# Graph network on one core: norms taken from columns in the node stages, and one difference for both exponents in the edge scan

## What is computed

```python
f = h + EPS
f = f * CLIP / jnp.maximum(CLIP, _norm(f))
fn = _norm(f)
p = jnp.tanh(fn) * f / fn
p = p + EPS
p = p * CLIP / jnp.maximum(CLIP, _norm(p))
Mp = p @ W
pn = _norm(p)
atan_norm = jnp.arctanh(jnp.clip(sqrt_c * pn, -0.9, 0.9))
t = Mp * atan_norm / pn / sqrt_c
t = t * clip2 / jnp.maximum(clip2, _norm(t))
tn = _norm(t)
hh = jnp.tanh(sqrt_c * tn) / sqrt_c / tn * t
...
g = hh + EPS
g = g * CLIP / jnp.maximum(CLIP, _norm(g))
gn = _norm(g)
log_h = jnp.arctanh(jnp.clip(sqrt_c * gn, -0.9, 0.9)) * g / gn
```

```python
seg_max = jax.ops.segment_max(logits, target, num_segments=m)
e = jnp.exp(logits - seg_max[target])
denom = jax.ops.segment_sum(e, target, num_segments=m)
out = jax.ops.segment_sum(e / denom[target] * (w3[source] + d), target, num_segments=m)
```

## Time and profile before

| what | value |
| --- | --- |
| time, median of 3 runs | 3100.99 us (3099.07 to 3108.09) |
| the profiled execution | 3096.49 us, its span 3094.6 us |
| `hyperbolic_nodes` | 563.0 to 666.4 us of the span |
| `end_hyperbolic` | 1293.2 to 1334.1 us |
| `edge_softmax` | 1619.0 to 2790.5 us |
| `end_edges` | 2790.5 to 2872.0 us |
| DVE, PE, ACT, POOL busy over the span | 74%, 61%, 59%, 34% |
| SP's queue in 1700 to 2700 us, waiting for the row copies | 453.9 us in 88 waits, at most 7.6 |

### The profile page before, as it was taken

One profiled execution on the slowest core, in us unless ns is written; L12 is line 12 of the kernel. 1 busy time (PEld: TensorE's weight loads), 2 busy tenths in 40 slices (PEclk: granted clock), 3 DMA queues, 4 the chain that ended last, 5 costly groups with the idle time before them and its releaser, 6 DMA issues. The chain is left out here.

```text
span 3094.6 us, 39006 instructions
## 1 busy us (share of the span) xinstructions
PE 1888.4 (61%) x7042; PEld 1007.8 (33%) x7043; DVE 2296.7 (74%) x4650; ACT 1832.1 (59%) x2352; POOL 1044.7 (34%) x984
## 2 busy tenths in 40 slices
PE   3354555359798567548846666666666666650636
PEld 1122222223333222112233434343433344430636
DVE  4799999479999678768926777777777777775444
ACT  0166666338888444358927877777777777860010
POOL 1000000000000011013207777777777777753000
PEclk8689898555656699869957777777777777765868
DMA  2144444104544499425614555555555555551616
GB/s 84 41 148 147 147 143 143 59 32 164 185 172 177 196 364 373 191 90 209 231 30 146 168 165 166 162 171 166 166 156 170 164 167 161 166 147 29 265 56 223
DMA packets 288619, 490.59 MB, mean 159 GB/s; under 512 B 39166, under 2 KB 237646, under 8 KB 275718
## 3 DMA queue, kind: packets, MB, share of 16 engines
q1 hardware_dynamic: 254694, 394.56, 36.7%
q0 software_dynamic: 26688, 54.65, 7.4%
q10 hardware_dynamic: 7200, 40.96, 3.4%
HBM read 282.58 MB, written 209.91 MB: 159 GB/s over the span
## 5 line engine op out<-in xcount | busy, mean ns | idle before, releaser
L1794 POOL DMA_INDIRECT es_got<-w,es_idx x808 | 882.3, 1092 | 346.1 <-issue 342.4
L1929 PE MATMUL en_pv<-en_sq,avg 128*128 128x512 f32 x202 | 197.7, 1079 | 371.6 <-ACT en_sq L2036 371.6
L1391 PE MATMUL acc<-src_hot,dst_hot 128*128 128x401 f16 x1008 | 231.6, 382 | 186.7 <-DVE src_hot L1366 166.7
L1366 DVE TENSOR_SCALAR src_hot<-iota,col_key 128x400 f16<-128x400 f16 x1008 | 315.9, 313 | 0.0
L1364 DVE TENSOR_SCALAR dst_hot<-iota_blk,row_key 128x128 f16<-128x128 f16 x1008 | 247.4, 245 | 11.9 <-PE acc L1391 11.4
L803 PE MATMUL pd_dn<-hT,pd_lhs 66*128 66x512 f32 (+1 forms) x350 | 233.3, 845 | 23.0 <-DVE pd_top L906 18.2
L2064 ACT COPY es_rows<-es_rp 128x512 f32<-128x512 f32 x202 | 118.2, 585 | 171.7 <-PE es_rp L1911 170.4
L1992 DVE TENSOR_TENSOR es_lg<-es_dn,es_w2p 128x512 f32<-128x512 f32 x101 | 69.5, 688 | 198.1 <-PE es_w2p L1885 198.1
L1391 PEld LDWEIGHTS acc<-src_hot,dst_hot 128*128 128x128 f16 x1008 | 107.2, 106 | 311.4 <-issue 270.8
L1059 PE MATMUL ns_acc<-ns_w,ns_val 128*65 128x512 f32 (+1 forms) x350 | 156.2, 595 | 71.2 <-DVE ns_w L1019 71.2
L1420 ACT COPY cbuf<-acc 128x401 f32<-128x401 f32 x200 | 98.4, 492 | 146.7 <-PE acc L1391 112.8
(11 more groups left out here) (500 smaller groups left out, 4753.9 us busy)
## 6 DMA issues: line engine op xcount, KB each, us to landing
rows<-es_rows SPq DMA_DIRECT2D x202, 256.0 KB, 2.8
counts_part<-cbuf SPq DMA_DIRECT2D x50, 800.0 KB, 3.7
near<-pd_out SPq DMA_DIRECT2D x25, 1600.0 KB, 6.2
ns_near<-near SPq DMA_DIRECT2D x25, 1600.0 KB, 9.8
ns_cnt<-counts_part SPq DMA_DIRECT2D x25, 1600.0 KB, 6.7
ss_cnt<-counts_part SPq DMA_DIRECT2D x25, 1600.0 KB, 6.6
n_ct<-turned ACTq DMA_DIRECT2D x50, 800.0 KB, 6.0
top_plane<-es_mx SPq DMA_DIRECT2D x101, 256.0 KB
```

The source lines that it names most:

```text
L1366: TS(src_hot[:, s, i, 0:PART].unsqueeze(1), k["iota16"][:, 0:PART].unsqueeze(1), k["col_key"][:, bass.ds(BATCH * b + i, 1)], None, ALU.is_ ...
L1391: last = nc.tensor.matmul(flat[:, bass.ds(places[i], PART + 1)], dst_hot[:, s, i, :], src_hot[:, s, i, 0:PART + 1], start=False, stop=Fals ...
L1794: pool.indirect_dma_start(got[:, s, t, half * 2 * F:(half + 1) * 2 * F], None, d["w23"], bass.IndirectOffsetOnAxis(ap=idx[:, s, half, t:t ...
L1929: nc.tensor.matmul(pv[:, :], avg[:, :], sq[:, :], start=True, stop=True).then_inc(var, 1)
```

## The change

In the node stages a norm after a limit is no longer computed from the plane: it is the old norm times the limit's factor, and the norm of `p` is the tanh itself. So the plane isn't multiplied by the limit at all, and factors are gathered in columns (`by`, `at`) and applied once. EPS (1e-15) counts in the norms only as a floor where it is needed. PE starts turning at `p`; banks are handed over one by one, `turned`, `evac`, `prod`, `aug_turned` and `aug_evac` counting banks or groups. ACT copies the first plane of `aug` before the last logarithms, and the second behind them.

In the edge stage the scan takes the maximum first and adds the penalty of the next edge after it, so that what stands before each edge, `mx[0:BANK]`, is the maximum of its own node's earlier edges, or about -1e30. One difference lg - mx, its part below 0 and its part above 0 are the two exponents. `top_plane` now holds maxima without the last edge, so that `lg` is stored too (`lg_plane`), and `end_edges` takes the maximum of both at the seam, with one more load and one more gather. The flags are read one edge later, and have one more column.

```diff
@@ edge_tables, SP @@
-                sp.dma_start(d["starts"].rearrange("h (p e) -> (h p) e", e=NT), starts[:, :]).then_inc(stored, 16)
+                for h in range(2):
+                    sp.dma_start(d["starts"][h, 0:EP // 2].rearrange("(p e) -> p e", e=NT),
+                                 starts[h * F:(h + 1) * F, :]).then_inc(stored, 16)
+                    sp.dma_start(d["starts"][h:h + 1, EP // 2:EP // 2 + 1], starts[0:1, 0:1]).then_inc(stored, 16)
@@ hyperbolic_nodes, DVE @@
+                def limited(scale, norm, limit):
+
+                    then(TS(scale, norm, limit, None, ALU.max))
+                    then(V.reciprocal(scale, scale))
+                    then(TS(scale, scale, limit, None, ALU.mult))
+
+                def small_and_log(name):
+                    then(TS(y, pn, rc, None, ALU.mult))
+                    then(TS(y, y, 0.9, -0.9, ALU.min, ALU.max), name)
+                    artanh_small(nc, then, small, y, t1, t2)
+                    then(V.reciprocal(lim, pn))
+                    answered()
+                    artanh_pick(nc, then, at, y, lnp, lnm, small, t1)
+                    then(TT(at, at, lim, ALU.mult))
...
-                limit_norm(nc, then, v[:, :, :], nr, t1, CLIP)
-                norm_sq(nc, then, ss, v[:, :, :], sq, "fn_sq")
+                limited(by, nr, CLIP)
+                then(TT(pn, nr, by, ALU.mult), "fn")
+                then(V.reciprocal(t1, pn))
+                then(TT(by, by, t1, ALU.mult))
                 answered()
...
-                norm_sq(nc, then, ss, v[:, :, :], sq, "p_sq")
-                answered()
-                limit_norm(nc, then, v[:, :, :], nr, t1, CLIP)
-                norm_sq(nc, then, ss, v[:, :, :], sq, "pn_sq")
-                answered()
-                then(nc.vector.tensor_copy(pn, nr))
...
+                then(TT(by, by, th, ALU.mult))
+                then(TT(v[:, :, :], v[:, :, :], spread(by), ALU.mult))
+                then(TS(v[:, :, :], v[:, :, :], EPS, None, ALU.add), "p")
+
+                limited(by, th, CLIP)
+                then(TT(pn, th, by, ALU.mult))
+                small_and_log("y1")
...
                 for g in range(4):
+                    dve.wait_ge(prod, g + 1)
...
+                norm_sq(nc, then, nu, u[:, :, :], sq, "nu")
...
+                then(TS(v[:, :, :], u[:, :, :], EPS, None, ALU.add))
                 answered()
+                then(TS(nr, nr, EPS * F ** 0.5, None, ALU.max))
+                limited(by, nr, CLIP)
+                then(TT(pn, nr, by, ALU.mult))
+                small_and_log("y2")
@@ hyperbolic_nodes, ACT @@
+                logs("y1")
                 for i, (a, w) in enumerate(SPANS):
+                    act.wait_ge(turned, i + 1)
+                    nc.scalar.copy(vt[:, a:a + w], pt[0:F, i, 0:w]).then_inc(evac, 1)
+                root("t_sq")
+                act.wait_ge(dsem, at_["tn"])
+                nc.scalar.activation(th, pn, ACT.Tanh, scale=rc).then_inc(asem, 1)
+                root("nu", nu)
+                for i, (a, w) in enumerate(SPANS):
+                    act.wait_ge(aug_turned, i + 1)
+                    nc.scalar.copy(k["hT"][0:W66, 0, a:a + w], pt[0:W66, i, 0:w]).then_inc(aug_evac, 1)
+                logs("y2")
+                for i, (a, w) in enumerate(SPANS):
+                    act.wait_ge(aug_turned, NS + i + 1)
+                    nc.scalar.copy(k["hT"][0:W66, 1, a:a + w], pt[0:W66, i, 0:w]).then_inc(aug_evac, 1)
@@ end_hyperbolic, DVE @@
-                limit_norm(nc, then, v[:, :, :], nr, t1, c2lim)
-                norm_sq(nc, then, ss, v[:, :, :], t, "zn_sq")
...
+                then(nc.vector.tensor_tensor(zn, nr, t1, ALU.mult), "zn")
+                then(nc.vector.reciprocal(t2, zn))
+                then(nc.vector.tensor_tensor(t1, t1, t2, ALU.mult))
@@ edge_softmax, SP @@
+                    sp.wait_ge(lg_ready, c + 1)
+                    sp.sem_inc(passed, 1)
+                    sp.dma_start(d["lg_plane"][:, bass.ds(c * BANK, BANK)], lg[:, s, :]).then_inc(tops_stored[s], 16)
                     sp.wait_ge(max_ready, c + 1)
                     sp.sem_inc(passed, 1)
-                    sp.dma_start(d["top_plane"][:, bass.ds(c * BANK, BANK)], mx[:, s, 1:BANK + 1])\
+                    sp.dma_start(d["top_plane"][:, bass.ds(c * BANK, BANK)], mx[:, s, 0:BANK])\
                       .then_inc(tops_stored[s], 16)
                     if left >= 2:
-                        sp.wait_ge(pen_used, c + 1)
-                        sp.sem_inc(passed, 1)
                         load_penalty(h + 1, s)
@@ edge_softmax, DVE @@
                     dve.wait_ge(gathered[s], 16 * 2 * CT * h + 16 * 2 * CT)
+                    dve.wait_ge(tops_stored[s], 32 * h)
                     nc.vector.tensor_tensor(lg[:, s, :], dn[:, s, :], w2p[:, :], ALU.subtract).then_inc(lg_ready, 1)
...
-                    nc.vector.tensor_tensor_scan(mx[:, s, 1:BANK + 1], pen[:, s, :], lg[:, s, :],
-                                                 mx[:, o, BANK:BANK + 1], ALU.add, ALU.max).then_inc(max_ready, 1)
+                    nc.vector.tensor_tensor_scan(mx[:, s, 1:BANK + 1], lg[:, s, :], pen[:, s, :],
+                                                 mx[:, o, BANK:BANK + 1], ALU.max, ALU.add).then_inc(max_ready, 1)
...
-                    nc.vector.tensor_tensor(e[:, s, :], lg[:, s, :], mx[:, s, 1:BANK + 1], ALU.subtract).then_inc(e_in, 1)
-                    nc.vector.tensor_tensor(dec[:, s, :], pen[:, s, :], mx[:, s, 0:BANK], ALU.add).then_inc(pen_used, 1)
-                    dve.wait_ge(pen_used, c + 1)
-                    nc.vector.tensor_tensor(dec[:, s, :], dec[:, s, :], mx[:, s, 1:BANK + 1],
-                                            ALU.subtract).then_inc(dec_in, 1)
+                    nc.vector.tensor_tensor(dec[:, s, :], lg[:, s, :], mx[:, s, 0:BANK], ALU.subtract).then_inc(rise, 1)
+                    dve.wait_ge(rise, c + 1)
+                    nc.vector.tensor_scalar(e[:, s, :], dec[:, s, :], 0.0, None, ALU.min).then_inc(e_in, 1)
+                    dve.wait_ge(e_in, c + 1)
+                    nc.vector.tensor_scalar(dec[:, s, :], dec[:, s, :], 0.0, None, ALU.max).then_inc(dec_in, 1)
@@ edge_softmax, ACT @@
-                    nc.scalar.activation(dec[:, s, :], dec[:, s, :], ACT.Exp).then_inc(dec_ready, 1)
+                    nc.scalar.activation(dec[:, s, :], dec[:, s, :], ACT.Exp, scale=-1.0).then_inc(dec_ready, 1)
@@ end_edges @@
+                sp.dma_start(lasts[:, 1:3], d["lg_plane"][:, EP // 2 - 2:EP // 2]).then_inc(loaded, 16)
...
+                then(TT(tops[:, :], tops[:, :], lasts[:, :], ALU.max))
```

210 lines of the change are left out of this document (87 added, 123 removed).

## The result

The changed kernel took 3004.73 us, median of 4 runs (2996.25 to 3009.41), beside 3103.02 for the kernel before on the same chip: a ratio of 0.969, with a 95% interval of 0.9666 to 0.9714. That is 98 us less, where 83.5 were forecast. The forecast of 3018 lies 13 us above it. The stated range of 3005 to 3050 begins at this median, to 0.3 us; the forecast's own part of it, 3008 to 3032, does not reach down to it, and rival 4's 3000 to 3008 holds it. The profiled execution took 2996.25 us, the shortest of the four.

What follows compares the result with a forecast made beforehand. Bound by a chain of hand-overs in the node stage and a closed 11.37 us ring per edge step. -46.7 - 7.1 - 31 + 1.3 = -83.5 from 3096.5 gives 3013, plus 4.5 for the median: 3018 us, range 3005 to 3050.

Steps and rivals of the forecast that it cites:

- rival 4: More gained than forecast: full clock for 9 us of matmul, gathers locking one place earlier; 3000 to 3008, chance 0.07.
- Node stage: hyperbolic_nodes: column norms and bank-by-bank hand-overs save 46.7 us, as 7.4 + 16.6 + 6.9 + 15.8.
- The next part: Node stage, from p to the end of the first product: earlier turn, hidden copies and products; 16.6 us gained.
- The third part: Node stage, limit and tanh with scale, treated as the first part: 6.9 us gained.
- The fourth: Node stage, from product aug[0] to the last copy into hT: 26.8 us becomes 11.0, gain 15.8.
- Hyperbolic end: End of the hyperbolic layer: same edit with norm, limit and tanh, 7.1 us less.
- Edge stage: Edge loop: 100 steps at 0.34 us less, minus 3 for steps with a late gather: 31 us less.
- the ring on DVE and ACT: Edge step from lg to next lg: two 0.43 us single-input operations bring dec's exponent 0.34 us sooner; ring 11.03 us.
- Rival 1: Edge stage: the gathers take the freed time, edge gain 0 to 18 us, total 3031 to 3049; chance 0.15.
- The 0.68 us of slack: Edge stage: spare time between last gather and lg, 5.15 against 4.47 needed; the shorter ring takes 0.34 of it.
- Rival 5: Edge stage: the two new operations wait for a gather in progress, up to 0.94 us each; 3200, chance 0.03.
- Rivals 2 and 3: Single-input operations take 0.69 us, 3059, chance 0.04; node stage keeps more of its chain, 3023 to 3028, chance 0.04.

Runs made afterwards that it cites:

- e1: The kernel before with only the two node functions (hyperbolic_nodes, end_hyperbolic) of the changed kernel: 3042.73 us, ratio 0.9822.
- e4: The changed kernel once more, unchanged: 3006.04 us, ratio 0.9694.
- e5: The changed kernel with the two single-input operations given a tile of zeros as second input: 3061.39 us, ratio 0.9872.
- e11: e3 with DVE's wait for the gathered rows also moved ahead of its wait for PE's turn: 3001.08 us, ratio 0.9681.
- e2: The changed kernel with the two node functions of the kernel before, so the edge part alone: 3057.69 us, ratio 0.9874.
- e12: The kernel before once more, unchanged: 3102.02 us, ratio 1.0.
- e6: The changed kernel without the store of lg in every step, its load and its gather at the seam: 2997.79 us, ratio 0.966.
- e7: The changed kernel with node-stage hand-overs made once per whole plane, column norms kept: 3015.55 us, ratio 0.972.
- e3: The changed kernel with DVE's wait for the stored planes placed ahead of its other waits before lg: 3000.12 us, ratio 0.9666.
- e8: e3 with ACT's copy of the counts moved behind the square: 3070.81 us, ratio 0.9899.
- e10: e3 with four gathers a step instead of eight, zeros for the second half: 2971.28 us, ratio 0.957.
- e9: e8 with four gathers a step instead of eight, zeros for the second half: 2917.48 us, ratio 0.9398.

## Why the forecast was right, and where its sizes were off

**Node stage, 46.7 forecast, 46.7 to 52.2 measured.** Point by point in the profile after: `p` ends 7.1 us sooner within the stage (7.4). The next part, to the end of the first product, gained 19.4 and not 16.6: 27.9 us after the stage's start for 54.4, less the 7.1. The term that was mis-sized is the matmul, which I had kept at its 9.00: it took 5.81, at full clock, and the copies' 3.2 went as forecast. The third part gained 7.1 (6.9). The fourth gained 15.1 (15.8), since the last copy into `hT` no longer ends it: that copy ends at 620.04, and DVE's line, which I had ending beside it, at 621.4. Together 48.7.

That sum is of one pair of profiles. The same products took 5.79 to 5.81 in six profiles with the new stage (the stage 54.6 to 55.3) and 8.25 to 8.49 in four others (e1, e4, e5, e11; the stage 56.6, and so the 46.7 of the forecast against 103.3). The old stage took 103.3, 104.2 (e2) and 106.8 (e12), with products of 9.00, 10.93 and 10.84. That full clock could be granted had stood in the bounds, as plus or minus 4. What decides it from one execution to the next, no run here shows.

**Hyperbolic end, 7.1 forecast, 6.4 to 7.5 measured. End of the edges, +1.3 forecast, +1.5 measured.** e6 takes the extra gather away and has 1.4 back.

**Edge stage, 31 forecast, 35 to 42 measured (e4, e2, e7, after) against the 1171.4 of before and e1, 31 to 37 against the 1167.1 of e12.** The step of the forecast that held is the ring on DVE and ACT: 0.43 us for the single-input operations, 1.72 instead of 2.06 to the exponent of `dec`, 0.34 a step. e5 undoes just this and loses more than all of it. Three terms that I didn't have lie beside it. First, DVE's new wait, costed at nothing because the store ends long before, still takes 0.10 of every step where it stood, between the turn and `lg` (e3): about 10 us by the marks, of which the medians of e3 and e4 show 6 without resolving it. Its cover was judged by when the store lands; the price is the wait itself. Second, 10 to 15 more steps at full clock, each 0.6 to 0.67 shorter: 6 to 10 us back, in the new order only. Third, the steps at full clock and the long steps became shorter themselves. In the first two profiles, with the shares of before: 81 x 0.26 + 11 x 0.57 = 27.6 from the ring, 15 x 0.65 = 9.8 from the clock, 7 x (13.4 - 12.8) = 4.5 from the long steps, together 41.9 of 41.7. In e4 the same sum has some 24 and 6. So that the forecast of 31 came this near is partly luck: two errors stand against each other, -10 for the wait and +10 for the clock.

**The gathers.** Rival 1 (0.15) did not come: PE waited for `es_got` in 11 to 13 turns (after, e2, e4, e7; 16 in e6), and in 15 to 17 with the old edge stage (before, e12, e1). What stood against it came true: POOL's line got shorter with the ring, since DVE holds it less, and from the last gather's end to the turn there are 4.18 us in the median step, after 3.86. The 0.68 us of slack were read from two steps, and they are no fixed number: in the steps of the kernel before where PE waited, the turn began 2.5 to 4.3 us after the last gather's end, and in the one of the earlier trace rows 3.1. e8, shorter by another 0.8 at the square, is what rival 1 describes, and shows how little room there was. I had argued from eight gathers at 10.0 us without a hold. With holds they need more: in the kernel after POOL was busy 845.1 us for 808 of them, 1.046 each, so (1.046 + 0.303) x 8 = 10.8 us a step, against a period of 11.0. In every kernel with eight gathers, 800 of the 807 gaps between them are 0.30 us long. So but for seven pauses (below) POOL is never idle, and only the holds fit its line to the ring: 1.22 us a step before, 0.85 after, 0.73 in e11. In e8 they were 1.53, and (1.132 + 0.303) x 8 = 11.5 us a step, with a ring of 10.7. There the scan of `s1`, and in some steps that of `s0`, hold a gather that they seldom held before. That is read from the trace of e8; no run moved those scans away from the gathers.

**Rival 5** is out: not one of the 101 operations of either kind is longer than 0.428, though 100 of the 101 at L2022 began while a gather was in progress. The Trainium skill (SBUF — State Buffer, section SBUF: two separate sides) has the exclusion hold whichever of the two starts first; here the DVE operations kept their length over gathers in progress, while the gather at 1960.63 took 1.85 instead of 0.94, some 0.75 past the scan's end at 1961.72. The trace disagrees with the page in one direction. **Rival 4** (0.07) is what came in the end, with a median inside its 3000 to 3008: for its first reason, full clock, in the node stage's matmuls in some executions, and in a place that it didn't name, the edge's variance. **Rivals 2 and 3** are out by the rows above: 0.43 for the operations, and a node stage of 54.6 to 56.6.

**What stays open.** What makes the clock rise more often in the new edge stage. A shorter period alone isn't it: 2 steps of 90 at a period of 11.50 (e5), 8 to 11 at 11.31, 21 to 26 at 11.0, 24 at 10.90 (e3), 36 at 10.76 (e10), 39 at 10.71 (e11), but 5 of 99 at 10.21 (e9) and 6 of 53 in e8, both with the square and the variance moved ahead of the counts' copy. And what makes POOL pause seven times, which gives the seven long steps (below).

## What to carry to other kernels

Where a loop is a closed ring over several engines, look at each wait between the last arrival and the operation that it releases: one that was met long ago still cost 0.09 to 0.10 us there, and it left that path when it was placed ahead of the late one. A shorter ring is worth its size only as long as the engine that is never idle beside it (here POOL, 10.8 of 11.0 us) has room; take the sum of its work with its holds, not without them, before cutting further. Handing over in pieces can bring more than the idle time that it removes: here the matmuls behind it were granted 0.66 to 1.00 of the clock in ten profiles, and 0.50 to 0.62 in four with the pause ahead of them. Take such a gain from more than one profile, since the same kernel gave 8.5 and 5.8 us.
